# One core, two layers over eight images: other places for ScalarE's pieces of work in the attention layer, for the residual sums, and exponentials turned by two engines

## What is computed

```python
# layer 0, per image: four depthwise 7-tap filters (across, down, two diagonals)
feats = stack([dw(x, w_h), dw(x, w_v), dw(x, w_d45), dw(x, w_d135)])
context = mean(feats * feats)                       # over the points
attn = softmax(leaky_relu(context @ w_att1.T, 0.2) @ w_att2.T)   # over the four
y = conv3x3(sum(attn * feats), w_proj)
# layer 1, per image: attention over channels, N = 96 * 96 points
q, k, v = split(w_qkv x);  q, k = softmax over the points
out = w_proj (context(k, v) applied to q)
qf = ifft2(w_q2 gelu(w_q1 Re fft2(x))).real
kf, vf = split(dwconv3x3(w_kv out))
attnf = softmax(l2norm(qf) l2norm(kf)^T * temperature)
y = w_projf (attnf vf)
```

## Time and profile before

| | |
|---|---|
| runs | 3883.29, 3883.88, 3897.43 us; median 3883.88 us |
| profiled execution | 3878.01 us, of it 3876.4 us span from first to last instruction |
| busy share | PE 85%, PEld 68%, DVE 68%, ACT 40%, POOL 23% |
| granted TensorE clock, mean | 0.930 of full speed |
| chain that ended last | PE 47%, DVE 16%, DMA 15%, issue 9%, POOL 5%, ACT 4% |

### The profile page before, as it was taken

The page is one execution under the profiler, slowest core; times in us unless marked ns, Lnnn a source line. Parts: engine busy times, 40 slices in busy tenths (PEclk is TensorE's granted clock), DMA queues, the critical chain, the costliest instruction groups (busy, mean ns, idle before and its releaser), DMA issues.

```text
span 3876.4 us, 55809 instructions
## 1 busy us (share of the span) xinstructions
PE 3284.9 (85%) x19102; PEld 2643.4 (68%) x19102; DVE 2636.5 (68%) x2943; ACT 1536.4 (40%) x2991; POOL 901.2 (23%) x1337
## 2 busy tenths in 40 slices
PE   4567989778998889869898798987899878988998
PEld 2355769657687577757777476875768757776867
DVE  7967777687857778577785777768785777854020
ACT  4412762136511564126631266203652156411540
POOL 1011322205122051211422132220512205121112
PEclk8778999889999899989999899988999889999999
DMA  5494236922478134862359423692237823483013
GB/s 128 109 227 109 71 82 151 237 69 68 93 169 206 50 85 99 210 158 56 79 111 241 105 71 85 146 240 69 70 91 168 206 52 80 104 201 101 1 38 65
DMA packets 222595, 455.89 MB, mean 118 GB/s; under 512 B 137408, under 2 KB 138640, under 8 KB 220240
## 3 DMA queue, kind: packets, MB, share of 16 engines
q1 hardware_dynamic: 169680, 268.83, 29.0%
q0 software_dynamic: 41472, 142.35, 16.2%
q10 hardware_dynamic: 11136, 40.81, 4.5%
HBM read 198.00 MB, written 155.71 MB: 91 GB/s over the span
## 4 chain that ended last, share of the span: by engine, by line
PE 47%; DVE 16%; DMA 15%; issue 9%; POOL 5%; ACT 4%; SPq 2%; ACTq 1%; DVEq 0%; POOLq 0%
DMA feat<-feats_d 10%; PE banks L1143 7%; PE banks L1131 7%; DVE feat L870 6%; PE banks L1113 6%; PE banks L1114 6%; POOL z L496 4%; PE banks L1172 3%; PE banks L1149 3%; PE banks L1195 3%; PE banks L1150 3%; PE banks L1185 3%; DMA feat<-in_x 2%; PE banks L1120 2%; DVE feat L991 2%
## 5 line engine op out<-in xcount | busy, mean ns | idle before, releaser
L870 DVE SCALAR_TENSOR_TENSOR feat<-xin,wt,feat 128x1152 f32<-128x1152 f32 x1116 | 1527.1, 1435 | 324.5 <-ACT feat L614 322.6
L1113 PE MATMUL banks<-e_hi,wp_a 128*96 128x384 f32 x1728 | 623.5, 361 | 175.7 <-DVE x L948 140.1
L1114 PE MATMUL banks<-e_lo,wp_b 128*96 128x384 f32 x1728 | 616.1, 357 | 0.0
L496 POOL COPY z<-vrow 96x192 f32<-96x192 f32 x384 | 397.0, 1070 | 765.9 <-ACT vrow L673 764.6
L1113 PE MATMUL banks<-e_hi,a_a 128*96 128x384 f32 x1656 | 562.9, 340 | 0.0
L1114 PE MATMUL banks<-e_lo,a_b 128*96 128x384 f32 x1656 | 560.8, 339 | 0.0
L1113 PEld LDWEIGHTS banks<-e_hi,wp_a 128*96 128x96 f32 x1728 | 301.5, 174 | 226.5 <-DVE x L948 121.1
L466 POOL DMA_DIRECT2D ring<-e_hi x576 | 293.0, 533 | 651.7 <-PE banks L1120 424.2
L1143 PEld LDWEIGHTS banks<-mats,z 96*96 96x96 f32 x3072 | 303.9, 173 | 95.7 <-issue 53.9
L1143 PE MATMUL banks<-mats,z 96*96 96x96 f32 x3072 | 307.7, 257 | 43.7 <-POOL z L496 40.9
L1114 PEld LDWEIGHTS banks<-e_lo,wp_b 128*96 128x96 f32 x1728 | 301.6, 175 | 30.3
(11 more groups left out here) (168 smaller groups left out, 4681.9 us busy)
## 6 DMA issues: line engine op xcount, KB each, us to landing
feat<-feats_d SPq DMA_DIRECT2D x224, 432.0 KB, 7.5
feats_d<-feat SPq DMA_DIRECT2D x160, 432.0 KB, 4.0
ring<-e_hi POOLq DMA_DIRECT2D x576, 97.2 KB, 4.7
feat<-in_x SPq DMA_DIRECT2D x64, 432.0 KB, 9.3
feats_d<-feat SPq DMA_DIRECT2D x192, 144.0 KB, 2.1
res<-in_x POOLq DMA_DIRECT2D x96, 288.0 KB, 5.7
out<-x POOLq DMA_DIRECT2D x96, 288.0 KB, 3.8
out<-res POOLq DMA_DIRECT2D x96, 288.0 KB, 4.7
```

What stands on the lines that cost most here:

```text
L496: pool.tensor_copy(z[:, :, 2 * g:2 * g + 2], vrow[:, g % VROWS, :, 0:C].rearrange("p r c -> p c r")).then_inc(z_turned, 1)
L870: dve.scalar_tensor_tensor(out=dst, in0=src, scalar=wt[:, q % VARIANTS, d * KT + k:d * KT + k + 1], in1=dst, op0=ALU.mult, op1=ALU.add).th ...
L1113: pe.matmul(dst, wa[:, t, :], rows_l(e_hi, a0, n, dx), start=(t == CENTRE_FIRST[0]), stop=False)
L1114: pe.matmul(dst, wb[:, t, :], rows_l(e_lo, a0, n, dx), start=False, stop=False)
```

## The change

Seven edits. (1) LEAD goes from 8 to 9: units 2 to 9 are tapped ahead of attention_weights instead of 2 to 8, units 1 to 7 have places in ScalarE's stages instead of 1 to 6, and 8 and 9 come whole after the second transform instead of 7 and 8. (2) FIRST_UNIT goes from 25 to 3: all placed pieces stand 22 nominal microseconds earlier. (3) GpSimd turns only the 24 pieces with even g; for odd g ScalarE makes the exponential a second time, from PSUM straight into z in turned order. ScalarE waits on z_turned only at even g, TensorE for 24 copies instead of 48. (4) HID_AT goes from 7 to 6: the alternation of copies and fg_high begins a tile earlier, and two copies stand together once. (5) hidden stands at tile 5's second half and logits at tile 6's first, instead of tile 7's first and second. (6) The hooks for residual sums stand after taps 2, 5, 8 and 11 of unit 0 and tap 2 of unit 1, instead of 2, 6 and 10 and then 2 and 6. (7) The indices of edit 4.

```diff
@@ -70,14 +70,14 @@
-LEAD = 8
+LEAD = 9
 LEAD_TAPS = TAPS // 2
...
-HID_AT = 7
-FIRST_UNIT, UNIT_TIME = 25.0, 17.2
+HID_AT = 6
+FIRST_UNIT, UNIT_TIME = 3.0, 17.2
@@ -490,7 +490,7 @@
-                    for g in range(U_KV):
+                    for g in range(0, U_KV, 2):
@@ -667,9 +667,11 @@
             def kv_rows(i):
                 for g in range(U_KV):
                     ps = stage(i, AT_KV + g)[0:W, 0:4 * C].rearrange("p (r c) -> p r c", c=2 * C)
-                    if g >= VROWS:
-                        act.wait_ge(z_turned, i * U_KV + g - VROWS + 1)
+                    if g >= VROWS and g % 2 == 0:
+                        act.wait_ge(z_turned, i * (U_KV // 2) + (g - VROWS) // 2 + 1)
                     act.activation(vrow[:, g % VROWS, :, 0:C], ps[:, :, 0:C], ACT.Exp)
+                    if g % 2:
+                        act.activation(z[:, :, 2 * g:2 * g + 2], ps[:, :, 0:C].rearrange("p r c -> p c r"), ACT.Exp)
@@ -783,7 +785,7 @@
-                    copies(min(NG, HID_AT + ch), min(NG, HID_AT + 1 + ch) if ch < NCH - 1 else NG)
+                    copies(min(NG, HID_AT + ch + (ch >= 4)), min(NG, HID_AT + 1 + ch + (ch >= 3)) if ch < NCH - 1 else NG)
@@ -1007,8 +1009,8 @@
-                taps(b, 0, hooks=[(2, between), (6, between), (10, between)])
-                taps(b, 1, 0, EARLY_TAPS, hooks=[(2, between), (6, between)])
+                taps(b, 0, hooks=[(2, between), (5, between), (8, between), (11, between)])
+                taps(b, 1, 0, EARLY_TAPS, hooks=[(2, between)])
@@ -1138,7 +1140,7 @@
-                                pe.wait_ge(z_turned, (i + 1) * U_KV)
+                                pe.wait_ge(z_turned, (i + 1) * (U_KV // 2))
@@ -1278,7 +1280,7 @@
-                    attention_block(b - 1, {(HID_AT, 0): hidden, (HID_AT, 1): logits} if first else {})
+                    attention_block(b - 1, {(HID_AT - 1, 1): hidden, (HID_AT, 0): logits} if first else {})
```

## The result

| | before | changed |
|---|---|---|
| median of four runs each | 3883.59 us | 3785.48 us (3781.37 to 3788.67) |
| ratio, 95% interval | | 0.9739 [0.9715, 0.9762] |
| profiled execution | 3878.01, span 3876.4 | 3788.67, span 3787.1 |
| granted TensorE clock, mean | 0.930 | 0.932 |

A forecast was written before the change was run, and what follows sets the result against it. Bound: GpSimd's copies in the kv stage, VectorE's start of the combination after the attention weights. Gains of 15.5 + 7.7 = 23.2 us a step, 162 in seven, took 3878.0 to 3716; plus 5.9, forecast 3722 us, range 3690 to 3790.

The forecast's parts named there:

- penalty for crossing lines: kv stage, ScalarE's extra exponential into z: crosses 16-byte lines twice as often, dearer by an unstated amount; 0.23 us each taken (0.21 to 0.38).

## What to carry to other kernels

The mean duration of an operation on GpSimd beside a busy VectorE holds only for the pauses that VectorE had in that trace; a change that makes VectorE gapless has to be priced also with the first such operation held until VectorE's next pause, and with whoever stands behind it. Where buffers join three engines in a ring, compare the longest single hold with what the buffers cover, not the sum with the stage. And when a change has lost part of its gain, look for the one long row before the many: pauses of 0.12 us after every second of VectorE's taps, or one operation of 0.06 us at the right place, gave 62 to 64 us here.

## What the runs showed of the hardware

**A copy on GpSimd can be held across many VectorE instructions.** 12.14 us over nine taps of 1.33 us, each with two inputs from SBUF; 13.53 with small one-input operations between them. Otherwise, as for the later copies of the stage, the two engines alternate: such a copy takes up to 1.6 us instead of 0.38, and the taps stand 1.46 us apart instead of 1.33. The Trainium skill, "SBUF — State Buffer" (section "SBUF: two separate sides"), has the shared port pair as an exclusive lock that whichever operation starts first holds for its whole instruction, while the other fully blocks. By that a copy would wait for the rest of one tap, at most 1.33 us; the alternating copies agree (1.61 - 0.38 = 1.23), the held ones do not, and here the measurement decides. Nor does a tap with a copy behind it take 1.33 + 0.38 = 1.71 us, but 1.46.

**A write in turned order costs ScalarE no time between starts.** L674 writes 192 numbers as 96 runs of two, and stands 0.21 us apart from its neighbours, just as L672 and L675, which write whole rows (a row of it is 386 ns long in the mean of the stage, theirs 373 and 377). The penalty for crossing lines that the prediction weighed (the Trainium skill, "SBUF — State Buffer", passage on SBUF cachelines) is not to be seen at this rate.
